# First layer: counting steps of TensorE between halves of turns and look-ups, messages two groups ahead

## What is computed

```
def _L0_gnn_ref(r, e, a):            # r nodes, e edge features, a = (src, dst)
    r1 = r[a[:, 0]] * e
    r2 = r[a[:, 1]] * e
    out = segment_sum(r1, a[:, 1])   # at the target
    out = out + segment_sum(r2, a[:, 0])   # at the source
    return out
x = layernorm(x + _L0_gnn_ref(x, edge_attr_128, ...))
```

## Time and profile before

| | before |
|---|---|
| three runs, us | 2382.91, 2379.21, 2386.02 |
| median, us | 2382.91 |
| profiled execution, us | 2381.67 |
| its span, first to last instruction, us | 2379.6 |
| mean granted TensorE clock | 0.72 of full |
| busy share: PE, DVE, POOL, ACT | 65%, 59%, 56%, 30% |
| chain of work that ended last | PE 36%, POOL 20%, issue 14%, DVE 10% |

### The profile page before, as it was taken

One profiled execution on the slowest core, in us unless ns is written; L12 is line 12 of the kernel. 1 busy time (PEld: TensorE's weight loads), 2 busy tenths in 40 slices (PEclk: granted clock), 3 DMA queues, 4 the chain that ended last, 5 costly groups with the idle time before them and its releaser, 6 DMA issues.

```text
span 2379.6 us, 41543 instructions
## 1 busy us (share of the span) xinstructions
PE 1549.5 (65%) x7809; PEld 1069.1 (45%) x7813; DVE 1394.0 (59%) x4832; ACT 714.3 (30%) x1272; POOL 1342.8 (56%) x1329
## 2 busy tenths in 40 slices
PE   3135777766776777776888544665556653796994
PEld 3034444444443444443777523554445553453552
DVE  8636766766766766777677755545555455425224
ACT  0001555554554555555000012222122221231230
POOL 0067777777777777777777437777777771000000
PEclk9978666666666666665899765656556566898997
DMA  1333444444444444444898422222222222232320
GB/s 44 70 91 93 128 122 121 125 117 117 126 125 117 129 124 116 127 131 128 220 250 230 130 53 54 53 53 52 52 52 54 51 51 106 97 148 94 145 97 27
DMA packets 332397, 251.06 MB, mean 106 GB/s; under 512 B 105217, under 2 KB 306541, under 8 KB 328619
## 3 DMA queue, kind: packets, MB, share of 16 engines
q1 hardware_dynamic: 224523, 118.11, 17.9%
q0 software_dynamic: 42240, 86.08, 13.5%
q10 hardware_dynamic: 65440, 45.04, 6.0%
HBM read 172.45 MB, written 78.22 MB: 105 GB/s over the span
## 4 chain that ended last, share of the span: by engine, by line
PE 36%; POOL 20%; issue 14%; DVE 10%; ACT 4%; DMA 3%; ACTq 2%; DVEq 2%; SPq 1%; POOLq 0%
POOL shared L822 18%; PE PS L999 11%; PE PS L899 8%; PE PS L872 6%; PE PS L884 4%; ACT PS L1158 3%; PE PS L863 2%; DMA shared<-record 2%; POOL G L810 2%; DVE shared L1621 2%; DVE shared L1560 2%; ACT shared L1164 1%; ACTq L1171 1%; DVE X L1681 1%; SPq L684 1%
## 5 line engine op out<-in xcount | busy, mean ns | idle before, releaser
L796 POOL DMA_INDIRECT record<-shared,IX x440 | 457.9, 1041 | 185.0 <-issue 161.5
L822 POOL DMA_INDIRECT shared<-table,src_of x440 | 439.6, 999 | 188.1 <-issue 133.8
L899 PE MATMUL PS<-shared 128*128 128x400 bf16 x816 | 298.9, 463 | 181.9 <-ACT PS L1158 154.7
L782 POOL DMA_INDIRECT G<-in_x_dram,MET x264 | 269.3, 1020 | 200.3 <-DMA MET<-meta_d 120.1
L1158 ACT ACTIVATE PS<-PS,kept 128x400 f32<-128x400 f32 x407 | 231.0, 568 | 221.9 <-PE PS L899 207.6
L1164 ACT ACTIVATE shared<-PS 128x400 uint16<-128x400 f32 x408 | 205.5, 504 | 125.8 <-issue 124.5
L1621 DVE TENSOR_SCALAR shared<-iota_h,shared 128x400 bf16<-128x400 f16 x816 | 238.2, 333 | 0.0
L1079 PE MATMUL PS<-shared,G 128*128 128x128 f32 x880 | 213.3, 389 | 18.2 <-issue 6.9
L872 PE MATMUL PS<-X,OHT 128*128 x880 | 207.0, 410 | 4.4 <-issue 2.6
L872 PEld LDWEIGHTS PS<-X,OHT 128*128 128x128 f32 x880 | 180.8, 306 | 64.3 <-issue 64.3
L899 PEld LDWEIGHTS PS<-shared 128*128 128x128 bf16 x816 | 64.0, 108 | 317.4 <-issue 200.7
(11 more groups left out here) (326 smaller groups left out, 2343.0 us busy)
## 6 DMA issues: line engine op xcount, KB each, us to landing
nearby<-shared ACTq DMA_DIRECT2D x408, 100.0 KB
shared<-in_edge_attr_dram SPq DMA_DIRECT2D x616, 64.0 KB
shared<-nearby SPq DMA_DIRECT2D x28, 1400.0 KB, 8.6
shared<-record SPq DMA_DIRECT2D x110, 258.0 KB, 3.4
MET<-meta_d SPq DMA_DIRECT2D x440, 2.0 KB
record<-shared,IX POOLq DMA_INDIRECT x440
shared<-table,src_of POOLq DMA_INDIRECT x440
G<-in_x_dram,MET POOLq DMA_INDIRECT x264
```

Source lines behind the costliest of these rows:

```text
L782: pool.indirect_dma_start(G[:, d, j, 0:D], None, x[:, :], row_index(MET[:, q, j, SRC - D:SRC - D + 1].bitcast(U32))).then_inc(a.gather[d], 16)
L796: pool.indirect_dma_start(record2[:, :], row_index(IX[:, q, j:j + 1]), M[:, g, j, :], None, bounds_check=SLOTS - 1, oob_is_err=False).then ...
L822: pool.indirect_dma_start(G2[:, half, GROUP * q + j, :], None, table1[:, :], row_index(src_of[:, GROUP * n + j:GROUP * n + j + 1])).then_i ...
L899: t = pe.matmul(PS[:, bank_, 0:HI], LOW[:, g, h, :], VIN[:, g, h, :], start=False, stop=h == 1, skip_group_check=True)
```

## The change

PE's turn and look-up of a group are each cut in two halves of two tiles; the order on PE becomes half turn of q + 3, s0, other half, s1, half look-up of q + 2, s2, other half, s3, sum of q. ACT copies the turned q + 3. DVE makes places and one-hots of q + 4 and source messages of q + 2. The last part of `places`, which makes `IX`, becomes `put_places`, at q + 2, with a wait for the scatters that used `IX` before. `M` gets a ring of five. The diff:

```
--- before.py
+++ after.py
@@ -283,8 +283,8 @@
         OHF = ring(DEEP, P)
         R, OH = S, OHF
         RL = ring(4, P)
-        M = ring(SIDES, ROW2)
-        M1 = ring(SIDES, D)
+        M = ring(DEEP, ROW2)
+        M1 = sb("M1", [P, SIDES, GROUP, D])
         OHTB = sb("OHTB", [P, SIDES, GROUP * P], BF16)
         src_of = sb("src_of", [P, TILES], U32)
         dloc = sb("dloc", [P, TILES])
@@ -412,7 +412,7 @@
                 self.put = [sem(f"{name}_put{g}") for g in range(put)]
 
 
-        a = Sems("a", "onehot turned onehot_t looked_up scaled summed added", load=DEEP, gather=DEEP, put=SIDES)
+        a = Sems("a", "onehot turned onehot_t looked_up scaled summed added", load=DEEP, gather=DEEP, put=DEEP)
         c = Sems("c", "onehot summed", load=DEEP)
         l = Sems("l", "scaled summed", load=4, gather=4)
 
@@ -685,8 +685,8 @@
 
                 def load_records2(i, q):
                     if isinstance(i, int) and i == 0 and q == 0:
-                        for g in range(SIDES):
-                            sp.wait_ge(a.put[g], 16 * TILES // SIDES)
+                        for g in range(DEEP):
+                            sp.wait_ge(a.put[g], 16 * TILES // DEEP)
                         sp.wait_ge(a.scaled, FULLS)
                     freed(sp, c.summed, i, q, DEEP)
                     sp.dma_start(S[:, q % DEEP, :, 0:ROW2], slots2[:, tiles(i, q), :]).then_inc(c.load[q % DEEP], 16)
@@ -783,7 +783,7 @@
                                             row_index(MET[:, q, j, SRC - D:SRC - D + 1].bitcast(U32))).then_inc(a.gather[d], 16)
 
             def put_messages(i, q):
-                g = q % SIDES
+                g = q % DEEP
                 pool.wait_ge(s_put_at, 2 * i + q // MANY + 1)
                 pool.wait_ge(s_m2, group(i, q) + 1)
                 later = (i + (q + 3) // TURN, (q + 3) % TURN)
@@ -859,18 +859,31 @@
                 g, n = q % SIDES, group(i, q)
                 pe.wait_ge(a.onehot, n + 1)
                 freed(pe, a.onehot_t, i, q, SIDES)
-                for j in range(GROUP):
+                for j in range(GROUP // 2):
+                    pe.transpose(PS[:, g, j * P:(j + 1) * P], OH[:, q % DEEP, j, :], ident[:, :])
+
+            def turn_a_rest(i, q):
+                g = q % SIDES
+                for j in range(GROUP // 2, GROUP):
                     t = pe.transpose(PS[:, g, j * P:(j + 1) * P], OH[:, q % DEEP, j, :], ident[:, :])
                 t.then_inc(a.turned, 1)
 
+            look_regs = []
+
             def look_up(i, q):
                 g, n = q % SIDES, group(i, q)
-                regs = columns(PE, columns_of[0], n)
+                look_regs[:] = columns(PE, columns_of[0], n)
                 pe.wait_ge(a.onehot_t, n + 1)
                 freed(pe, s_m2, i, q, SIDES)
-                for j in range(GROUP):
+                for j in range(GROUP // 2):
+                    pe.matmul(PS[:, 2 + g, j * P:(j + 1) * P], OHT[:, g, j * P:(j + 1) * P],
+                              X[:, bass.ds(look_regs[j], D)], start=True, stop=True)
+
+            def look_up_rest(i, q):
+                g = q % SIDES
+                for j in range(GROUP // 2, GROUP):
                     t = pe.matmul(PS[:, 2 + g, j * P:(j + 1) * P], OHT[:, g, j * P:(j + 1) * P],
-                                  X[:, bass.ds(regs[j], D)], start=True, stop=True)
+                                  X[:, bass.ds(look_regs[j], D)], start=True, stop=True)
                 t.then_inc(a.looked, 1)
 
             def sum_a(i, q):
@@ -914,7 +927,8 @@
                     if again(i):
                         sum_step(step_no(i, q, s))
                 return body
-            pipeline(pe, (turn_a, 2), (step_pe(0), 0), (look_up, 1), (step_pe(1), 0), (sum_a, 0), (step_pe(2), 0), (step_pe(3), 0),
+            pipeline(pe, (turn_a, 3), (step_pe(0), 0), (turn_a_rest, 3), (step_pe(1), 0), (look_up, 2), (step_pe(2), 0),
+                     (look_up_rest, 2), (step_pe(3), 0), (sum_a, 0),
                      (prepare_pe, 0))
             for k in range(STEPS - 8, STEPS):
                 sum_step(fixed(k))
@@ -1183,7 +1197,7 @@
                 if again(i):
                     store_step(step_no(i, q, PER - 1))
             act.wait_ge(s_dest, 16)
-            pipeline(act, (copy_turned, 2), (step_act(0), 0), (step_act(1), 0), (step_act(2), 0), (step_act(3), 0), (last_store, 0))
+            pipeline(act, (copy_turned, 3), (step_act(0), 0), (step_act(1), 0), (step_act(2), 0), (step_act(3), 0), (last_store, 0))
             for k in range(STEPS - 8, STEPS):
                 if k + 1 < STEPS:
                     seed_next(fixed(k))
@@ -1521,6 +1535,16 @@
                 dve.tensor_copy(src_of[:, bass.ds(GROUP * n, GROUP * MANY)], flat(MET[:, at, :, SRC - D]))
                 dve.wait_ge(s_dl, turn + 1)
                 dve.tensor_copy(dloc[:, bass.ds(GROUP * n, GROUP * MANY)], flat(DL[:, at, :]))
+
+            def put_places(i, q):
+
+                if q % MANY:
+                    return
+                at, turn = slice(q, q + MANY), 2 * i + q // MANY
+                dve.wait_ge(s_dl, turn + 1)
+                if again(i):
+                    for d in range(DEEP):
+                        dve.wait_ge(a.put[d], 16 * GROUP * (turn - 1))
                 dve.tensor_scalar(inside[:, :, :], DL[:, at, :], 0.0, None, ALU.is_ge).then_inc(s_in, 1)
                 dve.wait_ge(s_in, 2 * turn + 1)
                 dve.scalar_tensor_tensor(outside[:, :, :], DL[:, at, :], float(P), inside[:, :, :],
@@ -1542,12 +1566,12 @@
 
             def source_messages(i, q):
                 g, d, n = q % SIDES, q % DEEP, group(i, q)
-                if used(i, q, SIDES):
-                    dve.wait_ge(a.put[g], 16 * GROUP * use(i, q, SIDES))
-                dve.tensor_copy(M[:, g, :, D:ROW2].bitcast(I32), MET[:, q, :, SRC_IN_BLOCK - D:SRC_IN_BLOCK - D + 1])
+                if used(i, q, DEEP):
+                    dve.wait_ge(a.put[d], 16 * GROUP * use(i, q, DEEP))
+                dve.tensor_copy(M[:, d, :, D:ROW2].bitcast(I32), MET[:, q, :, SRC_IN_BLOCK - D:SRC_IN_BLOCK - D + 1])
                 dve.wait_ge(a.load[d], 16 * GROUP * (use(i, q, DEEP) + 1))
                 dve.wait_ge(a.looked, n + 1)
-                dve.tensor_tensor(M[:, g, :, 0:D], PS[:, 2 + g, :].rearrange("p (j f) -> p j f", f=D),
+                dve.tensor_tensor(M[:, d, :, 0:D], PS[:, 2 + g, :].rearrange("p (j f) -> p j f", f=D),
                                   R[:, d, :, 0:D], ALU.mult).then_inc(s_m2, 1)
 
             def target_rows(i, q):
@@ -1626,7 +1650,7 @@
                     if again(i):
                         build_step(step_no(i, q, s + 2))
                 return body
-            pipeline(dve, (places, 3), (onehots_a, 3), (step_dve(0), 0), (source_messages, 1), (step_dve(1), 0), (target_rows, 0), (step_dve(2), 0),
+            pipeline(dve, (places, 4), (onehots_a, 4), (step_dve(0), 0), (put_places, 2), (source_messages, 2), (step_dve(1), 0), (target_rows, 0), (step_dve(2), 0),
                      (target_messages, 0), (step_dve(3), 0), (prepare, 0))
             for k in range(STEPS - 6, STEPS):
                 build_step(fixed(k))
```

## The result

The changed kernel takes 2495.2 us against 2381.1 (medians of four runs), where 2489 us was forecast. One of its four runs fell in a slow state (2590.3 us at a mean clock of 0.62, the others at 0.70 to 0.71); without it the median is 2493.3 us, a ratio of 1.047 with a 95% interval of 1.044 to 1.051, so slower by 112 us. The profiled execution spans 2491.5 us against 2379.6. All that follows compares with 2493.3.

What follows compares the result with a forecast made beforehand. The prediction took a ring of PE, ACT and DVE as the bound. +1.17 us a group times 100 gave +117, less 6 and 5: +106 on 2381.7, 2488, median 2489 us; forecast 2452 to 2520, wider range 2418 to 2558.

Steps and rivals of the forecast that it cites:

- What bounds before: First layer's loop, 8.95 us a group: a ring of PE, ACT and DVE sets the pace; nobody waits for GpSimd.
- Its floor of 8.5 us: GpSimd's busy time plus 0.30 us before each indirect DMA, 759 us for 89 groups: 8.5 us a group.
- the turning point of the hardware loop (8.8): Rival that GpSimd is the true bound: 8.5 + 0.3 for the loop's turning point, 2362 us; chance 0.06.
- The two hops: New PE waits: ahead of s1 for ACT's copy and seed, 1.34 us; ahead of s3 for DVE's build, 1.54 us.
- Lower level: Changed loop at 1.2 GHz: full group 10.88 us, late group (no sum) 9.48, mean 10.32 against 9.30.
- Upper level: Changed loop at 2.4 GHz: 7.86 us a group against 7.1.
- ACT's 2.28 us bounds both kinds: At 2.4 GHz, ACT free for the copy 2.28 us after s3's end limits full and late groups; s1 at 3.98 us.
- The clock: PE in the loop: share of time at 2.4 GHz falls from 0.28 to 0.15, giving 9.86 us a group, +1.29.
- 0.12: Loop's turning point hides more of itself behind the new ACT wait: -0.12 us a group.
- PE's unbroken stretches: PE's work without a hole shrinks from 5.3 us to 4.4 (full) and 3.6, so the upper clock share falls.
- The ends: Last groups lack turns and look-ups, late gathers start earlier: -5 us together; the first turn's start: -6 us.
- Lead and ring: Messages two groups ahead and ring of five: nothing in the loop, -6 us in the first turn.

Runs made afterwards that it cites:

- relieving it: Two of four gather tiles of a full group became plain SyncE loads of the first 128 node rows, in the kernel before: 2381.7 us.
- the filled kernel: Three matmuls of zeros put by PE into each of its two holes, ahead of s1 and ahead of s3, in the changed kernel: 2374.6 us.
- seed first: ACT does seed and rounding of s0 ahead of copy_turned, all else as in the changed kernel: 2469.9 us.
- both first: ACT's seed and rounding of s0 ahead of copy_turned and DVE's build of s3 ahead of source_messages, in the changed kernel: 2332.8 us.

## Why the prediction was right

**What bounds before.** Right. Nobody waited for GpSimd, and relieving it changed nothing. Its floor of 8.5 us was right too, and was reached (8.44). That GpSimd would in addition lose the turning point of the hardware loop (8.8) was wrong: in the reordered kernel its longest wait is 0.30 us.

**The two hops.** Right in place and size: 1.38 and 1.58 us in the trace, 1.34 and 1.54 by hand. Undoing the DVE one alone gives back 140 us.

**Lower level.** 10.32 us a group by hand; the two stretches above are 0.1 us shorter than their hand sums, the second with s1 and part of a half look-up at the upper level.

**Upper level.** Mis-sized: 7.86 us was too short for full groups. At the upper level the filled kernel takes 614.49 - 605.85 = 8.64 us after a full group. The step that failed is "ACT's 2.28 us bounds both kinds". After a full group s1 comes 4.51 us after s3's start, not 3.98, because DVE does target messages and then the build of s1: a third hop, which the forecast doesn't have. Another 0.25 us lies between s1 and s2 (1.59 instead of 1.34), where PE waits for DVE again. The third hop in the changed kernel itself, DVE and then PE:

```profile
602.14 1.57 DVE L1596 TENSOR_TENSOR acc<-PS,acc 128x128 f32 x4 [1.64 <-PE PS L897]
603.63 0.42 DVE L1642 TENSOR_TENSOR shared<-iota_b,shared 128x256 bf16<-128x256 bf16 x1
603.98 0.55 DVE L1645 TENSOR_SCALAR shared<-iota_h,shared 128x400 bf16<-128x400 f16 x2
```

```profile
604.58 0.51 PE L912 MATMUL PS<-shared 128*128 128x400 bf16 x2 [1.77 <-DVE shared L1645]
```

At the lower level it lies just beside ACT's: s1 comes at 5.58 us in the changed kernel, released by ACT, and at 5.47 in "seed first", released by DVE. So it costs nothing there. It is also in the waits of after: 132 waits for L1645 in 79 groups, more than one per group. After late groups the step was right, as the filled kernel shows at the upper level:

```profile
707.11 0.51 PE L912 MATMUL PS<-shared 128*128 128x400 bf16 x2 [0.94 <-DVE shared L1652]
...
711.09 0.50 PE L912 MATMUL PS<-shared 128*128 128x400 bf16 x2 [1.26 <-ACT PS L1179]
...
714.96 0.51 PE L912 MATMUL PS<-shared 128*128 128x400 bf16 x2 [0.94 <-DVE shared L1652]
```

s1 comes at 3.98 us and the next s3 at 7.85. The mean of both kinds is then 8.33.

**The clock.** The direction was right, the share not: 0.60 is 20% of the time at the upper level, not 15%. With 20% and 8.33 the sum gives 0.80/10.32 + 0.20/8.33 = 0.1015, 9.85 us, or +1.28 - 0.12 = +1.16 against 1.13 measured. With the forecast's own upper level it would have been +1.02. One error makes the forecast too slow (the share) and the other too fast (the upper level); they nearly cancel, so the 2489 is better than its parts. The same sum with the upper share kept at 28% gives 0.72/10.32 + 0.28/8.33 = 0.1034, 9.67 us, +0.98: by this estimate some 18 of the 112 us are the clock's fall, and the rest are the holes themselves at the clock of before.

The forecast took the share from PE's unbroken stretches. That reading was too simple, as the kernel before shows right behind the stretch it rests on:

```profile
610.57 0.82 PE L899 MATMUL PS<-shared 128*128 128x400 bf16 x2 [0.84 <-ACT PS L1158]
611.19 1.06 PE L863 MATMUL PS<-ident,shared 128*128 128x128 f32 x4
612.24 0.82 PE L899 MATMUL PS<-shared 128*128 128x400 bf16 x2
612.96 2.07 PE L872 MATMUL PS<-X,OHT 128*128 x8
614.88 0.83 PE L899 MATMUL PS<-shared 128*128 128x400 bf16 x2
616.55 0.82 PE L899 MATMUL PS<-shared 128*128 128x400 bf16 x2 [0.84 <-ACT PS L1158]
```

PE is busy without a hole from 610.57 to 615.71 us, as it was from 601.5 to 606.7, and the next steps stay at the lower level (0.82). That the share came out near the forecast is in part luck.

**The ends.** The start gained 4.0 us (6 forecast). From the last product to the late gathers it is 1.6 us won of the 2.4 counted on; the rest of the 5 us did not show. What follows the loop took 5 us longer. Why stays open; over all kernels run, the time from the last target rows to the end lay between 1265 and 1276 us (before 1268, changed 1272).

**Lead and ring.** "Nothing in the loop" was nearly right: 8.86 against 8.95. In the reordered kernel the lead was expected to be worth 30 to 50 us:

> The kernel before with PE's halves and both reorderings (seed ahead of copy_turned, build of s3 ahead of source_messages), but the leads and the ring of two of before. Against the same with messages two groups ahead (2333 us). Theory: with the compute ring no longer the bound, GpSimd is, and now its waits for the messages count: it waits for source_messages after every group without a gather, and loses its turning point of some 3 us in ten groups, so 0.3 to 0.5 us a group more: 2360 to 2385 us. Rival (lead is worth nothing here too): 2333 us.

It was worth about 9 us (2341.5 against 2332.8, intervals of the ratios that touch). In its trace, 300 to 1100 us, GpSimd waits 14.1 us for source messages in 9 places, and DVE 15.3 us for scatters in 11; both are gone with the lead and the ring, and both are small. The expected wait after every group without a gather is not there: the messages are early enough one group ahead.

## What to carry to other kernels

When one engine's order is cut finer, read the other engines' lists at the same spot: an item that waits for the second half must stand behind everything that the first engine needs before it. Here moving one item in DVE's list was worth 140 us. After that, test for two bounds of the same height by removing both; each alone looks like nothing. And where TensorE works in pieces with short holes, its clock is part of the price of each hole.

## What the runs showed of the hardware

TensorE's granted clock followed the filling of its holes more strongly than expected (0.75 and 0.85 or more). In the changed loop, with holes mostly of 0.4 to 1.7 us, it got the upper level (2.4 GHz) a fifth of the time; with three matmuls of zeros in each of two holes a group the mean was 0.94 of full, and in the kernel before, with one hole filled, 0.91 instead of 0.64. That is 119 and 44 us for work that is thrown away. The Trainium skill (TensorE: Matmul & The Clock Gate, Part 1) says that sustained activity releases the throttle; these runs agree, and show that matmuls of zeros count as activity.

GpSimd's indirect DMAs of 128 rows took 1.01 to 1.04 us each (the mean over 300 to 1100 us, by kernel), with 0.30 us before each one even where GpSimd waited for nobody; in "both first" 603 of them filled 797 of 800 us.
